# Moving a recurrence and half of an MLP from channels to tokens, and folding gate scores into other products, in a two-phase Trainium2 kernel

## Chip, cores and metric

The kernel runs on one core of a Trainium2 chip. The metric is the device time of one execution in microseconds (us), lower is better. "Granted clock" is the share of TensorE's full speed that the chip let it have; its two levels are 1.2 and 2.4 GHz, shown as 0.5 and 1.0.

## What is computed

The input is 16 x 56 x 56 tokens of 96 channels (50,176 tokens, fp32). The reference, cut to what matters:

```
x0 = x
x  = ln(x)                                  # over channels, no weights
w  = ln(x) * ln1_w + ln1_b                  # tokens in windows of 7x7 = 49 steps
h  = w[step] @ Bm + h @ A                   # recurrence over the 49 steps of a window
xr = h @ Cm
y  = gelu((ln(xr)*ln2_w + ln2_b) @ W1 + b1) @ W2 + b2     # 96 -> 384 -> 96
x2 = x0 + xr + y
t  = ln(x2)
scores = t @ gate_w + gate_b                # 4 experts, the two largest are kept
out = x2 + sum over the two kept experts of weight_e * (gelu(t @ w1_e + b1_e) @ w2_e + b2_e)
```

## The kernel before

**Phase 1** walks over 49 tiles; tile t holds step t of all 1,024 windows (8 groups of 128 tokens), so the recurrence runs from tile to tile. Five engines run queues that are written out by hand as loops over `periods()`; period p works on several tiles at once: the MLP of tile p, state and `xr` of tile r = p + 1, the input of tiles p + 2 and p + 3, gate and sorting of tiles p - 1 and p - 2. An engine takes its queue strictly in order, so a wait holds all that is behind it.

Per tile, in the kernel before:

- DVE takes moments of x (`moments(LN_X)`), POOL makes 1/sqrt(variance) with a `pow` (`rstd_of`, L396), ACT normalises x by tokens (L476), PE turns it to channels (`to_channels`, L878), ACT copies it out (L530).
- PE sums the new state by channels: `from_state` (L917, A) and `from_input` (L924, Bm), 2 products of 512 columns each; ACT copies it to `h_t` (L510). `sum_xr` (L931) multiplies it by Cm with tokens on the partitions, in 8 products; DVE copies `xr` out (L728), takes moments, normalises it (L626), PE turns it, ACT rounds it to `y_hi` (L501) and DVE makes the rest `y_lo` (L702). `y_hi` and `y_lo` are the two fp32r parts that `up` needs.
- `up` (L890 to L892) makes 6 units of 512 columns, three products each; ACT applies gelu (L486); `down` (L901) sums the units by channels in fp32; ACT adds the bias (L493), `turn_y` (L909) turns the sum to tokens, `add_x2` (L636) adds `x + xr`.
- LN over x2: moments, POOL's `pow`, `normalise` on DVE (L626, written into the row), PE turns it (L878), ACT copies it (L523), and 8 products of 4 columns (L976) give the scores. `gate` picks the two experts, `positions` gives each row its place among the 6 pairs of experts, and POOL scatters the rows to DRAM with 8 indirect DMAs (L405). A row is x2, t, the scores below the largest, and the token's number: 197 words.

**Phase 2** reads the sorted rows in 103 blocks of 512 tokens with one pair of experts each: turn t to channels (L1006), 6 units of `up2` (L1020 to L1022), gelu, `down2` (L1034 to L1036), turn back (L1043), combine (L833), scatter the result (L437).

Of the kernel before, what the change touches and what calls it, by code (L numbers as in the profile page):

```python
# [6 lines left out]
F32R = mybir.dt.float32r  # L7
# [27 lines left out]
COL_X2, COL_T, COL_BELOW, COL_ID = 0, C, 2 * C, 2 * C + EXPERTS  # L35
# [18 lines left out]
X_RING = 5  # L54
G_RING = 4
# [15 lines left out]
FIRST_LOADS, LATER_LOADS = 5, 3  # L71
PREP_STEPS = 9
# [7 lines left out]
def periods():  # L80
    return range(-3, TILES + 2)
# [1017 lines left out]
```

## Time and profile before

| | us |
|---|---|
| three runs | 2190.02, 2192.92, 2193.45 (median 2192.92) |
| the profiled execution: its time | 2187.12 |
| its span (first to last instruction) | 2185.4 |
| busy: PE, PEld, DVE, ACT, POOL | 2036.4, 1435.5, 1609.1, 1467.4, 1523.1 |
| mean granted clock | 0.981 |

Times of rows in the trace count from the start of the span. PEld is PE's loading of the stationary operand. A fp32 product shows as two records, so "x16" stands for 8 fp32 products; the shown end of a PE record is modelled and lies past the start of the next. "[1.78 <-DVE y_lo L702]" is idle time ahead of a row and what ended it.

### The profile page before, as it was taken

Reading aid. Unit: us, or ns where it says so; the run is one execution under the profiler, and the core shown is the slowest. Engines: PE = TensorE matmul, PEld = TensorE weight load, DVE = VectorE, ACT = ScalarE, POOL = GpSimd, SP = SyncE. Lnnn points to the kernel's source line nnn. Section 1 sums busy time; section 2 is a strip of 40 time slices with the busy share of each in tenths; the row PEclk is TensorE's granted clock in tenths of the full one; section 3 lists DMA queues with packets and bytes.
Section 4 is the critical chain, followed back from the end, with each engine's and each line's share of the span. In section 5 each row is a group of like instructions: output and inputs, shape, how many; then the busy total and the mean of one; then the engine's idle time right before and its main releaser. Section 6 shows DMA issues by size and latency. Waiting matters only on the chain.

```text
span 2185.4 us, 39186 instructions
## 1 busy us (share of the span) xinstructions
PE 2036.4 (93%) x10145; PEld 1435.5 (66%) x10145; DVE 1609.1 (74%) x6863; ACT 1467.4 (67%) x2529; POOL 1523.1 (70%) x1389
## 2 busy tenths in 40 slices
PE   3999999999999999999966999999999999999996
PEld 2666665656666666666644777777777777777775
DVE  5777777777777777777754777777777777777775
ACT  3555555555454555555524888888888888898895
POOL 2366666666666666666553777778888887788876
PEclk9999999999999999999967999999999999999998
DMA  4111111111111121211116767766666677666663
GB/s 160 32 51 59 53 58 54 57 56 49 63 49 62 47 64 48 63 49 47 36 45 201 213 199 208 213 203 200 204 200 208 199 208 209 206 209 211 207 203 94
DMA packets 120722, 272.90 MB, mean 125 GB/s; under 512 B 25702, under 2 KB 34303, under 8 KB 120500
## 3 DMA queue, kind: packets, MB, share of 16 engines
q1 hardware_dynamic: 85680, 209.91, 32.8%
q0 software_dynamic: 32000, 58.87, 7.6%
q8 instruction: 84, 1.38, 0.3%
q10 hardware_dynamic: 2820, 1.61, 0.3%
q14 instruction: 138, 1.13, 0.2%
HBM read 204.28 MB, written 66.98 MB: 124 GB/s over the span
## 4 chain that ended last, share of the span: by engine, by line
PE 53%; POOL 20%; DVE 19%; issue 6%; ACT 1%; DMA 1%; ACTq 0%; SPq 0%; POOLq 0%; DVEq 0%
POOL rstd L396 10%; POOL sorted_rows L405 7%; PE mix_ps L1034 7%; PE mix_ps L1036 6%; PE mix_ps L1035 6%; DVE xr_n L626 4%; PE turn_ps L1020 3%; PE up_ps L1020 3%; PE turn_ps L1022 3%; PE up_ps L1021 3%; PE turn_ps L1021 3%; PE up_ps L1022 3%; DVE stats L614 3%; PE tok_ps L1043 3%; DVE y_lo L702 3%
## 5 line engine op out<-in xcount | busy, mean ns | idle before, releaser
L437 POOL DMA_INDIRECT out<-out_sb,idx x412 | 440.1, 1068 | 199.2 <-issue 125.3
L789 DVE TENSOR_TENSOR g_lo<-g,g_hi 128x512 fp32r<-128x512 f32 x618 | 418.4, 687 | 167.4 <-ACT g_hi L547 93.6
L405 POOL DMA_INDIRECT sorted_rows<-rows,pos x392 | 421.1, 1074 | 114.0 <-issue 99.9
L547 ACT CAST g_hi<-g 128x512 fp32r<-128x512 f32 x618 | 380.9, 616 | 13.1
L426 POOL TENSOR_TENSOR ex<-euler,rows 128x8 f32<-128x8 f32 x206 | 367.8, 1798 | 13.6 <-DMA rows<-sorted_rows 12.5
L486 ACT ACTIVATE g<-up_ps 128x512 f32<-128x512 f32 x294 | 175.7, 598 | 250.7 <-PE up_ps L892 135.9
L901 PE MATMUL y_ps<-g,d_raw 128*96 128x512 f32 x588 | 302.3, 609 | 0.2 <-ACT y_sb L493 0.2
L396 POOL TENSOR_TENSOR rstd<-var_eps,neg_half 128x8 f32<-128x8 f32 x147 | 248.4, 1689 | 12.2
L1034 PE MATMUL mix_ps<-g_hi,ew 128*96 128x512 f32 x618 | 246.5, 399 | 1.8 <-DVE g_lo L789 1.2
L393 POOL TENSOR_SCALAR var_eps<-moment 128x8 f32<-128x8 f32 x147 | 31.8, 216 | 307.2 <-DVE moment L620 293.5
L1036 PE MATMUL mix_ps<-g_lo,ew 128*96 128x512 f32 x618 | 244.4, 396 | 0.0
L1035 PE MATMUL mix_ps<-g_hi,ew 128*96 128x512 f32 x618 | 244.0, 395 | 0.0
L890 PE MATMUL up_ps<-y_hi,w_hi 98*128 98x512 f32 x294 | 185.6, 631 | 25.5 <-DVE y_lo L702 25.1
L541 ACT ACTIVATE g<-turn_ps 128x512 f32<-128x512 f32 x310 | 184.5, 595 | 27.5 <-PE turn_ps L1022 17.9
L541 ACT ACTIVATE g<-up_ps 128x512 f32<-128x512 f32 x308 | 183.3, 595 | 22.8 <-PE up_ps L1022 11.3
L626 DVE TENSOR_SCALAR xr_n<-xr,moment,rstd 128x96 f32<-128x96 f32 x392 | 98.3, 331 | 117.3 <-POOL rstd L396 117.3
L493 ACT ACTIVATE y_sb<-y_ps,b_col 96x512 f32<-96x512 f32 x98 | 67.0, 684 | 166.4 <-PE y_ps L901 162.2
L559 ACT ACTIVATE y_sb<-mix_ps,ew 96x512 f32<-96x512 f32 x206 | 140.7, 683 | 48.3 <-PE mix_ps L1036 38.3
L476 ACT ACTIVATE x_n<-x_in,shift,rstd 128x96 f32<-128x96 f32 x392 | 149.7, 455 | 0.0
L1020 PE MATMUL turn_ps<-y_hi,ew 98*128 98x512 f32 x310 | 137.5, 444 | 1.4 <-DVE y_lo L794 1.4
L1020 PE MATMUL up_ps<-y_hi,ew 98*128 98x512 f32 x308 | 135.6, 440 | 3.1 <-DVE pair_of L844 3.1
L1036 PEld LDWEIGHTS mix_ps<-g_lo,ew 128*96 128x96 f32 x618 | 99.8, 161 | 43.2
(159 smaller groups left out, 4426.1 us busy)
## 6 DMA issues: line engine op xcount, KB each, us to landing
ew<-expert_w SPq DMA_DIRECT2D x206, 384.0 KB
ew<-expert_w SPq DMA_DIRECT2D x206, 288.5 KB
rows<-sorted_rows SPq DMA_DIRECT2D x103, 394.0 KB
x_in<-in_x SPq DMA_DIRECT2D x49, 384.0 KB
out<-out_sb,idx POOLq DMA_INDIRECT x412
sorted_rows<-rows,pos POOLq DMA_INDIRECT x392
sorted_rows<-pad_rows SPq DMA_DIRECT2D x11, 394.0 KB, 10.6
expert_w<-w_hi SPq DMA_DIRECT2D x4, 192.0 KB, 2.1
```

The source lines that it names most:

```text
L396: pool.tensor_tensor(rstd[:, k, t % 2, :], var_eps[:, k, :], neg_half[:, :], ALU.pow).then_inc(rstd_ok[k], 1)
L405: pool.indirect_dma_start(out=sorted_rows[:, :], out_offset=bass.IndirectOffsetOnAxis(ap=pos[:, r, s:s + 1], axis=0), in_=rows[:, r, s, :] ...
L426: pool.tensor_tensor(ex[:, b % 2, s:s + 2, :], euler[:, :].rearrange("p (s e) -> p s e", s=2), rows2[:, b % IN_RING, s:s + 2, COL_BELOW:CO ...
L437: pool.indirect_dma_start(out=out_rows, out_offset=bass.IndirectOffsetOnAxis(ap=idx[:, r, s:s + 1], axis=0), in_=out_sb[:, r, s, :], in_of ...
L541: act.activation(g[:, n % G_RING, :], up_bank(n), ACT.Gelu).then_inc(gelu2_done, 1)
L547: act.copy(g_hi[:, n % PART_RING, :], g[:, n % G_RING, :]).then_inc(hi_done, 1)
L789: dve.tensor_tensor(g_lo[:, n % PART_RING, :], g[:, n % G_RING, :], f(g_hi[:, n % PART_RING, :]), ALU.subtract).then_inc(lo_done, 1)
L901: pe.matmul(y_ps[0:C, :], d_raw[:, k, :], g[:, n % G_RING, :], start=(k == 0), stop=(k == KB - 1)).then_inc(down_done, 1)
L1020: pe.matmul(up_bank(n), hi[0:KR, :], t_hi, start=True, stop=False)
L1034: pe.matmul(y2_bank(q), hi, g_hi[:, part, :], start=(k == 0), stop=False)
L1035: pe.matmul(y2_bank(q), lo, g_hi[:, part, :], start=False, stop=False)
L1036: pe.matmul(y2_bank(q), hi, g_lo[:, part, :], start=False, stop=(k == KB - 1)).then_inc(down2_done, 1)
```

## The change

1. **x in two layouts.** Beside `x` the program gets `x_chan`, the same values with channels on the partitions (384 KB more per tile, by SyncE, ring of 2). Mean removal is folded into the weights (`in_w` is the centred Bm, and centred gate weights as 4 more columns), so `from_input` multiplies raw x in 8 products of 100 columns, and ACT multiplies the result by 1/std (`scale_in`). The transpose of normalised x and its copy go.
2. **State by tokens.** One product per group (`h_t` stationary, `state_aug` = A, Cm and Cm times the gate weights, 196 columns) gives the part of the next state and `xr` together. DVE adds the input's part (`take_state`), PE turns the state (`turn_h`), ACT copies it (`copy_h`). All of it goes in halves of 512 tokens.
3. **`xr` normalised on ACT.** ACT copies `xr` from PSUM and normalises it (`normalise_xr`), DVE only makes `shift`; POOL's `pow` for x (tile p + 4) and for `xr` (tile p + 1) is one instruction on 128x16 that waits for both variances. The small `var_eps` step moves from POOL to DVE.
4. **`down` by tokens.** Gelu's output is the stationary operand, 4 products of 100 columns per unit; b2 enters by one fp32r product of 400 columns per half. The bias copy and `turn_y` go. `add_x2` reads the sum directly.
5. **Scores as four more columns** of the products of 1, 2 and 4. They are summed in `gate_sum` (three small steps on ACT and DVE per half) and multiplied by 1/std of x2 in `gate`. L976, its transpose and copy go; t isn't written any more. `positions` comes one period earlier.
6. **Rows of 103 words**: x2, scores, mean, 1/std, number. Phase 2 normalises the block's rows on DVE (`normalise(b)`, 4 instructions of 128x96) two blocks ahead.

The core of the diff:

```diff
-COL_X2, COL_T, COL_BELOW, COL_ID = 0, C, 2 * C, 2 * C + EXPERTS
+COL_X2, COL_BELOW, COL_MEAN = 0, C, C + EXPERTS
+COL_RSTD, COL_ID = COL_MEAN + 1, COL_MEAN + 2
@@ SyncE
+            for t in range(XT_RING, TILES):
+                if t + X_RING - XT_RING - 1 >= X_RING and t + X_RING - XT_RING - 1 < TILES:
+                    load_x(t + X_RING - XT_RING - 1)
+                load_x_t(t)
@@ POOL, loop over periods
+            for p in periods():
+                if tile(p - 2):
+                    scatter(p - 2, (1,))
+                if tile(p - 1):
+                    rstd_t(p - 1)
+                if tile(p - 2):
+                    scatter(p - 2, (2, 3))
+                if tile(p + 4) or tile(p + 1):
+                    powers_of_variance(p + 4, p + 1)
+                if tile(p - 2):
+                    scatter(p - 2, (4, 5, 6, 7))
+                if tile(p - 1):
+                    scatter(p - 1, (0,))
@@ ACT, r = p + 1
+            def scale_in(t, h):
+                act.wait_ge(in_done, 2 * t + h + 1)
+                if h == 0:
+                    act.wait_ge(rstd_ok, rstd_calls(t, t - 3) + 1)
+                if t >= 1:
+                    act.wait_ge(h_tok_ok, 2 * (t - 1) + h + 1)
+                for s in range(HALF_SUBS):
+                    ins = act.activation(x_b[:, HALF_SUBS * h + s, :], in_ps[:, s, 0:C], ACT.Identity,
+                                         scale=rstd[:, rstd_calls(t, t - 3) % 2, LN_X, HALF_SUBS * h + s:HALF_SUBS * h + s + 1])
+                ins.then_inc(x_b_ok, 1)
+                act.copy(gate_sum[:, t % GATE_RING, HALF_SUBS * h:HALF_SUBS * (h + 1), :], in_ps[:, :, C:CG]).then_inc(in_gate_ok, 1)
...
+                if tile(r):
+                    copy_xr(r, 0)
...
+                if tile(p + 3):
+                    scale_in(p + 3, 0)
+                if tile(p):
+                    gelu(p, 4)
+                if tile(r):
+                    normalise_xr(r, 0)
+                if tile(p + 2):
+                    copy_h(p + 2, 0)
+                    copy_h(p + 2, 1)
+                if tile(r):
+                    normalise_xr(r, 1)
+                if tile(p):
+                    gelu(p, 5)
...
+                if tile(p + 3):
+                    scale_in(p + 3, 1)
+                if tile(r):
+                    y_high(r, 0)
@@ DVE, r = p + 1
+            def take_state(t, h):
+                subs = slice(HALF_SUBS * h, HALF_SUBS * (h + 1))
+                dve.wait_ge(state_done, 2 * (t + 1) + h + 1)
+                if tile(t):
+                    dve.wait_ge(xr_copied, 2 * t + h + 1)
+                if tile(t + 1):
+                    dve.wait_ge(x_b_ok, 2 * (t + 1) + h + 1)
+                    if t >= 0:
+                        dve.wait_ge(h_turned, 2 * t + h + 1)
+                    dve.tensor_tensor(h_tok[:, subs, :].rearrange("p (b s) c -> p b s c", b=2), state_ps[:, :, :, 0:C],
+                                      x_b[:, subs, :].rearrange("p (b s) c -> p b s c", b=2), ALU.add).then_inc(h_tok_ok, 1)
...
+                if tile(p):
+                    y_low(p, 1)
+                if tile(p - 1):
+                    add_x2(p - 1, 1)
+                    rows_stats(p - 1, 1)
+                    variance(LN_T, p - 1, (rstd_t_ok, p - 1))
+                if tile(r) or r == -1:
+                    take_state(r, 0)
+                if tile(p + 4):
+                    t = p + 4
+                    dve.wait_ge(x_loaded[t % X_RING], 16 * (t // X_RING + 1))
+                    for h in range(2):
+                        half_stats(LN_X, t, h, x_in[:, t % X_RING, :, :])
+                    variance(LN_X, t, (rstd_ok, rstd_calls(t - 1, t - 4) + 1))
...
+                if tile(r):
+                    xr_stats(r, 0)
+                if tile(r) or r == -1:
+                    take_state(r, 1)
+                if tile(r):
+                    xr_stats(r, 1)
+                    variance(LN_R, r, (rstd_ok, rstd_calls(r + 2, r - 1) + 1))
+                if tile(p - 1):
+                    gate(p - 1)
+                if tile(r):
+                    n = rstd_calls(r + 3, r)
+                    dve.wait_ge(rstd_ok, n + 1)
...
+                if tile(p):
+                    add_x2(p, 0)
+                if tile(p - 1):
+                    positions(p - 1)
+                if tile(r):
+                    if r >= 2:
+                        dve.wait_ge(x2_ok, 2 * (r - 1))
+                    dve.tensor_tensor(x_xr[:, r % 2, :, :], xr[:, :, :], x_in[:, r % X_RING, :, :], ALU.add).then_inc(x_xr_ok, 1)
+                if tile(p):
+                    rows_stats(p, 0)
+                if tile(r):
+                    y_low(r, 0)
@@ PE
+                if k == 0:
+                    tok.take(pe, x2_ok, 2 * t + h + 1)
+                    pe.matmul(tok_ps[:, 0:HALF_SUBS * CG], ones_r[:, :], b2_parts[:, :], start=True, stop=False)
+                pe.wait_ge(gelu_done, n + 1)
+                for s in range(HALF_SUBS):
+                    ins = pe.matmul(mlp_ps[:, s, :], g[:, n % G_RING, sub(s)], d_mlp[:, k, :], start=False,
+                                    stop=(k == KB - 1 and s == HALF_SUBS - 1))
+                ins.then_inc(down_done, 1)
...
+            def from_state(t, h):
...
+                for s in range(HALF_SUBS):
+                    ins = pe.matmul(state_ps[:, s // 2, s % 2, :], h_t[:, sub(HALF_SUBS * h + s)], state_aug[:, :], start=True, stop=True)
+                ins.then_inc(state_done, 1)
@@ phase 2, DVE
+            def normalise(b):
+                dve.wait_ge(rows_loaded[b % IN_RING], 16 * (b // IN_RING + 1))
+                if b >= 2:
+                    dve.wait_ge(t_turned, b - 1)
+                for s in range(BSUBS):
+                    row = rows2[:, b % IN_RING, s, :]
+                    ins = dve.tensor_scalar(t_tok[:, b % 2, s, :], row[:, COL_X2:COL_BELOW], row[:, COL_MEAN:COL_RSTD],
+                                            row[:, COL_RSTD:COL_ID], ALU.subtract, ALU.mult)
+                ins.then_inc(t_tok_ok, 1)
...
+                    if u == 3 and b + 2 < BLOCKS:
+                        normalise(b + 2)
```

(In `from_state` h_t's group is the stationary operand and `state_aug` moves; `y_high(p, 1)`, gelu 0 to 2 and the copies of `xr` open ACT's period.)

On PE, before, the end of a period and the start of the next (transposes are MATMUL rows with `ident`):

```order
L878 MATMUL turn_ps<-ident,x_n 96x128 x8
L976 MATMUL tok_ps<-gate_aug,tn_t 128x4 x8
L901 MATMUL y_ps<-g,d_raw 96x512 x2
L878 MATMUL turn_ps<-ident,xr_n 96x128 x8
L909 MATMUL tok_ps<-ident,y_sb 128x96 x4
L917 MATMUL mix_ps<-h_t,a_raw 96x512 x2
L890 MATMUL up_ps<-y_hi,w_hi 128x512
```

The same place with the change, from the second `from_input` to the next period's first `up` and `from_state`:

```order
L1060 MATMUL y_ps<-in_w,x_t 128x100 x4
L1030 MATMUL turn_ps<-ident,xr_n 96x128 x4
L1051 MATMUL tok_ps<-d_mlp,g 128x100 x4
L1030 MATMUL turn_ps<-ident,xr_n 96x128 x4
L1051 MATMUL tok_ps<-d_mlp,g 128x100 x4
L1040 MATMUL up_ps<-y_hi,w_hi 128x512
```

The product of the state (L917), which stood between the transpose of `xr` and the next `up`, has moved behind the first two units of `up`; two units' `down` in four small products each stand around the second transpose.

On ACT, before, a whole period from the first two gelus:

```order
L486 ACTIVATE g<-up_ps 128x512 x2
L476 ACTIVATE x_n<-x_in,shift,rstd 128x96 x4
L510 COPY h_t<-mix_ps 96x1024
L486 ACTIVATE g<-up_ps 128x512 x2
L476 ACTIVATE x_n<-x_in,shift,rstd 128x96 x4
L493 ACTIVATE y_sb<-y_ps,b_col 96x512
L486 ACTIVATE g<-up_ps 128x512
L523 COPY tn_t<-turn_ps 96x1024
L486 ACTIVATE g<-up_ps 128x512
L530 COPY x_t<-turn_ps 96x1024
L493 ACTIVATE y_sb<-y_ps,b_col 96x512
L501 CAST y_hi<-turn_ps 96x1024
```

With the change, the second part of a period, from the fourth gelu to the rounding of `y_hi` (its two halves stand on one row, the first closes the period and the second opens the next):

```order
L530 ACTIVATE x_b<-y_ps,rstd 128x96 x4
L533 COPY gate_sum<-y_ps 128x16
L569 ACTIVATE g<-up_ps 128x512
L554 ACTIVATE xr_n<-xr,shift,rstd 128x96 x4
L538 COPY h_t<-turn_ps 96x512 x2
L554 ACTIVATE xr_n<-xr,shift,rstd 128x96 x4
L569 ACTIVATE g<-up_ps 128x512
L530 ACTIVATE x_b<-y_ps,rstd 128x96 x4
L533 COPY gate_sum<-y_ps 128x16
L562 CAST y_hi<-turn_ps 96x512 x2
```

Behind the wait for `shift` (first L554) there now stand eight more steps that `y_hi` has to wait for, among them a `scale_in`; before, only L501 stood behind the transpose of `xr_n`.

## Rows read from the trace of the kernel before

**Rows 1.** The page's first part: busy time, share of the span, instructions.

```profile
span 2185.4 us, 39186 instructions
PE 2036.4 (93%) x10145; PEld 1435.5 (66%) x10145; DVE 1609.1 (74%) x6863; ACT 1467.4 (67%) x2529; POOL 1523.1 (70%) x1389
```

**Rows 2.** Windows: start:end, length, busy us (records), clock, DMA share, GB/s.

```profile
60.00:1080.00 1020.00, 959.49 (x4895) 632.47 (x4896) 774.65 (x4176) 546.38 (x924) 657.32 (x678) 1.00 0.17 53
1190.00:2150.00 960.00, 958.74 (x4776) 724.63 (x4775) 736.44 (x2293) 851.52 (x1493) 779.17 (x596) 1.00 0.69 205
```

**Rows 3.** Timeline, PE: start, us, engine, line; `up` of tile 0 and tile 48.

```profile
50.04 0.50 PE L890 MATMUL up_ps<-y_hi,w_hi 98*128 98x512 f32 x1
...
1105.30 0.50 PE L890 MATMUL up_ps<-y_hi,w_hi 98*128 98x512 f32 x1 [1.78 <-DVE y_lo L702]
```

**Rows 4.** Waits from 60 to 1080: engine line, releaser, us, times, longest.

```profile
PEld up_ps L890 <- DVE y_lo L702: 62.7, 46, 1.4
```

**Rows 5.** Timeline of one steady period, PE.

```profile
611.11 1.04 PE L878 MATMUL turn_ps<-ident,x_n 128*96 128x128 f32 x8
612.09 1.95 PE L976 MATMUL tok_ps<-gate_aug,tn_t 97*128 97x4 f32 x16
...
621.12 0.40 PE L890 MATMUL up_ps<-y_hi,w_hi 98*128 98x512 f32 x1
621.36 0.39 PE L891 MATMUL up_ps<-y_lo,w_hi 96*128 96x512 f32 x1
622.18 1.94 PE L924 MATMUL mix_ps<-x_t,b_aug 97*96 97x512 f32 x4
627.07 1.92 PE L931 MATMUL mix_ps<-a_raw,h_t 96*128 96x96 f32 x16
```

**Rows 6.** Timeline, DVE: a gate, statistics, and `y_lo` of 512 columns.

```profile
616.46 0.17 DVE L646 COPY score<-tok_ps 128x32 f32<-128x32 f32 x1
618.61 0.53 DVE L636 TENSOR_TENSOR rows<-tok_ps,x_xr 128x384 f32<-128x384 f32 x1
625.43 1.34 DVE L614 BATCH_NORM_STATS2 stats<-x_in 128x6 f32<-128x96 f32 x8
626.81 0.64 DVE L620 BATCH_NORM_AGGREGATE moment<-stats 128x2 f32<-128x6 f32 x8
1166.88 0.69 DVE L794 TENSOR_TENSOR y_lo<-y_ps,y_hi 96x512 fp32r<-96x512 f32 x1 [15.84 <-ACT y_hi L553]
```

**Rows 7.** Timeline, ACT.

```profile
621.32 1.29 ACT L486 ACTIVATE g<-up_ps 128x512 f32<-128x512 f32 x2 [2.54 <-issue]
622.51 1.53 ACT L476 ACTIVATE x_n<-x_in,shift,rstd 128x96 f32<-128x96 f32 x4
1166.26 0.58 ACT L553 CAST y_hi<-y_ps 96x512 fp32r<-96x512 f32 x1 [29.48 <-PE y_ps L1006]
```

**Rows 8.** Timeline, POOL, and a DVE row inside its pair of powers.

```profile
2.42 0.74 POOL L369 MEMSET pad_rows<- 128x788 f32 x1
603.80 1.67 POOL L396 TENSOR_TENSOR rstd<-var_eps,neg_half 128x8 f32<-128x8 f32 x1
1154.85 0.96 POOL L405 DMA_INDIRECT sorted_rows<-rows,pos  x1 [0.30 <-issue]
1703.04 3.95 POOL L426 TENSOR_TENSOR ex<-euler,rows 128x8 f32<-128x8 f32 x2
1704.82 0.68 DVE L789 TENSOR_TENSOR g_lo<-g,g_hi 128x512 fp32r<-128x512 f32 x1
```

**Rows 9.** Timeline: last store of expert weights; phase 2's first transposes.

```profile
35.57 0.45 SPq L296 DMA_DIRECT2D expert_w<-b_col  x1
...
1165.14 1.09 PE L1006 MATMUL y_ps<-ident,rows 128*96 128x128 f32 x4 [10.90 <-DMA rows<-sorted_rows]
```

**Rows 10.** PE idle at 64.75, and the granted clock after 1105.30.

```profile
66.25 1.05 PE L878 MATMUL turn_ps<-ident,xr_n 128*96 128x128 f32 x8 [1.50 <-DVE xr_n L626]
```

**Rows 11.** Windows, PE alone: length, busy, clock, DMA share, GB/s.

```profile
1107.00:1108.00 1.00, 1.00 (x4) 0.50 0.00 0
```

More of the change, by code:

```diff
@@ L54 @@
 X_RING = 5
+XT_RING = 2
+GATE_RING = 6
 G_RING = 4
@@ new lines, in normalise_xr @@
+            def normalise_xr(t, h):
+                if h == 0:
+                    act.wait_ge(shift_ok, t + 1)
+                if t >= 1:
+                    act.wait_ge(xr_turned, 2 * (t - 1) + h + 1)
+                for s in range(HALF_SUBS * h, HALF_SUBS * (h + 1)):
+                    ins = act.activation(xr_n[:, s, :], xr[:, s, :], ACT.Identity, bias=shift[:, s:s + 1],
+                                         scale=rstd[:, rstd_calls(t + 3, t) % 2, LN_R, s:s + 1])
+                ins.then_inc(xr_n_ok, 1)
@@ L912, in from_state @@
-            def from_state(r):
-                mix.take(pe, h_t_ok, r + 1)
-                if r >= 1:
-                    pe.wait_ge(h_t_ok, r)
-                    for h in range(2):
-                        pe.matmul(mix_ps[0:C, half(h)], a_raw[:, 0, :], h_t[:, half(h)], start=True, stop=False)
-            def from_input(r):
-                pe.wait_ge(x_t_ok, r + 1)
-                if r == 0:
-                    pe.wait_ge(bias_rows, 48)
-                for h in range(2):
-                    ins = pe.matmul(mix_ps[0:C, half(h)], b_aug[:, :], x_t[:, half(h)], start=(r == 0), stop=True)
-                ins.then_inc(h_summed, 1)
@@ new lines, in down, with from_input @@
+                ins.then_inc(down_done, 1)
+            def from_input(t, h):
+                inp.take(pe, in_gate_ok, 2 * t + h + 1)
+                if h == 0:
+                    pe.wait_ge(x_t_loaded[t % XT_RING], 16 * (t // XT_RING + 1))
+                for s in range(HALF_SUBS):
+                    ins = pe.matmul(in_ps[:, s, :], x_t[:, t % XT_RING, sub(HALF_SUBS * h + s)], in_w[:, :], start=True, stop=True)
+                ins.then_inc(in_done, 1)
+            def from_state(t, h):
+                if t == -1 and h == 0:
+                    pe.wait_ge(bias_rows, 16 * 4)
+                if t >= 0:
+                    pe.wait_ge(h_t_ok, 2 * t + h + 1)
+                n = 2 * (t + 1) + h
+                if n >= 1:
+                    pe.wait_ge(h_tok_ok, min(n, 2 * TILES))
+                if n >= 3:
+                    pe.wait_ge(state_gate_ok, n - 2)
+                for s in range(HALF_SUBS):
+                    ins = pe.matmul(state_ps[:, s // 2, s % 2, :], h_t[:, sub(HALF_SUBS * h + s)], state_aug[:, :], start=True, stop=True)
+                ins.then_inc(state_done, 1)
@@ L941, in _ @@
                     up(p, 1)
-                if tile(p - 2):
-                    tok.take(pe, base_set, p - 1)
-                    pe.wait_ge(score_counted, p - 1)
-                    pe.matmul(tok_ps[:, 0:TYPES], earlier[:, :], count[:, :, SUBS - 1], start=True, stop=True)
-                    pe.matmul(tok_ps[:, TYPES:2 * TYPES], ones[:, :], count[:, :, SUBS - 1], start=True, stop=True).then_inc(
-                        ranked, 1)
-                if tile(r):
-                    from_input(r)
+                if tile(r) or r == -1:
+                    from_state(r, 0)
                 if tile(p):
```

471 lines of the change are left out of this document (241 added, 230 removed).

## Prediction

> **What bounds the kernel now.** First the page's busy shares: PE leads with 93% [rows 1]. Then the windows, to see whether that holds in both phases: in steady phase 1 PE is busy 959.49 of 1020 us and DVE only 774.65, in steady phase 2 PE is busy 958.74 of 960 with ACT next at 851.52; the clock is 1.00 in both [rows 2]. Then the timeline: `up` of tile 0 starts at 50.04 and that of tile 48 at 1105.30 [rows 3], so a period lasts 1055.3 / 48 = 21.98 us. The waits show how little PE idles in it: the largest, for `y_lo` ahead of `up`, is 62.7 us in 46 times, 1.4 us a period [rows 4]. So both phases go at PE's pace. A change that takes work from PE can shorten phase 1 until another chain takes over; phase 2 can only stay or get longer, since its PE work stays.
>
> **PE's work per period.** A fp32 product of 512 columns shows as two records, four records in 1.94 [rows 5], 0.43 each after the modelled tail. With tokens as the stationary operand, 16 records take 1.92 at 96 moving columns and 1.95 at 4 columns [rows 5]: 0.12 each whatever moves, so the loading sets it. Gone: four products of 512 columns for the state (3.5), six for `down` (5.2), Cm's 8 (1.9), the scores' 8 (1.95), three sets of 8 transposes at 1.04, `turn_y` (1.0): 16.7. New: 24 small products for `down` at two records (5.8), 8 `from_input` (1.9), 8 `from_state`, whose 196 columns I cost by columns, 2 x 0.43 x 196/512 = 0.33 each (2.6), two sets of transposes (2.1), b2 (0.4): 12.8. PE falls by about 3.9 to some 17.5 a period. PE would let phase 1 gain 48 x 4 = 190 us. It won't, since the order of waits now closes a longer loop over the other engines.
>
> **The loop that sets the new period.** Count from the moment at which half 0 of `y_lo` of tile p is there (0).
>
> - PE: two units of `up`, six products 0.24 apart [rows 5], 1.45; first half of `from_state` 1.3, seen 0.2 later: 2.95. DVE has done half 1 of `y_lo`, `add_x2`, statistics and variance of the rows by 2.7, so it waits here.
> - ACT copies half of `xr` (384 columns; 512 take 0.58 [rows 7]), 0.5: 3.5. DVE `take_state`: 0.53 for 384 columns as L636 [rows 6], and a small step 0.1: 4.2.
> - DVE, statistics of x for tile p + 4: 1.34 and 0.64 for the whole tile [rows 6], with one more stop between halves 2.1, variance 0.25: 6.55. Half of `xr`'s statistics 1.05, `take_state` 0.65, the other half 1.05, variance 0.25: 9.55.
> - POOL: the `pow` on 128x16, 3.15 (below): 12.75. Beside it runs `gate`: 2.15 before (616.46 to 618.61) [rows 6], with four small steps more and one less 2.55, so it ends at 12.1 and isn't what `shift` waits for. `shift` 0.25: 13.0.
> - ACT: half of `normalise_xr` 1.53 (as L476 [rows 7]), two `copy_h` of 0.6, other half 1.53, gelu 5 0.65 (two in 1.29 [rows 7]), `scale_in` 1.53 and 0.2, half of `y_hi` 0.6: 7.25, at 20.25.
> - DVE: half of `y_lo`, 0.69 [rows 6] and a handover: 21.05. PE starts the next `up` at 21.1.
>
> DVE's other work of the period (about 4 us between `shift` and `y_lo`, 15.6 in all) and ACT's 13.6 have room. POOL has 8 scatters of 0.96 plus 0.30 [rows 8], 10.1, and 1.67 + 3.15 of powers: 15, and comes to the 128x16 `pow` at about 7. So the loop, not a full engine, sets 21.1: 0.9 less than now, 48 x 0.9 = **-42 us**. Handing over in halves is what the change gains from, and the eight steps ahead of `y_hi` on ACT are what eats it.
>
> **The price of the 128x16 pow** isn't in the trace. Below it is bounded by 1.67 of the 128x8 one [rows 8] (nothing makes double the work cheaper), above by twice that, 3.34. POOL's plainest row takes 0.74 for 788 elements a partition [rows 8], so elements cost there, and little of 1.67 can be fixed cost; I take 3.15. At 1.67 the loop would close over `gate` instead, 0.65 earlier: 20.45.
>
> The Trainium skill (SBUF — State Buffer, "SBUF: two separate sides") says that VectorE and GpSimd share a port pair as an exclusive lock, held for the whole instruction, against a DVE instruction with two SBUF inputs. `gate` begins with such instructions right as the long `pow` starts. The row speaks against it: inside a pair of powers of 3.95 us a two-input DVE instruction took 0.68 [rows 8], where a wait for a power of nearly 2 would show. By the row the sum stays; by the rule it would be the third rival.
>
> **Start and end of phase 1.** Today the last of 20 stores of expert weights is issued at 35.57 [rows 9] and x for the first tiles is long there. Now x_t of tile 2 stands behind these stores in SyncE's queue, they start only after `later_weights`, which now stands behind the first `take_state` (about 33), and `from_input` of tile 2 stands ahead of the first transpose of `xr` on PE. That puts the first `up` at about 57: **+7 us** (between -2, if the stores come no later than today, and +12). At the other end 59.8 us lie between the last first `up` (1105.30) and phase 2's first transposes (1165.14) [rows 3, 9]. Normalising, transposing, copying and scoring the last tile go, and `positions` comes earlier; then POOL's queue is last: from about 10.5 on, 16 scatters at 1.26 and a `pow`, to 32.5, and as today 9.3 from its last scatter (1154.85 and 0.96 [rows 8]) to the transposes: 42, **-18 us** (-12 to -20).
>
> **Phase 2.** A block takes 9.8 us at PE's pace. `normalise` adds 1.0 to DVE's 7.5 (736.44 in 98 blocks [rows 2]). It stands two blocks ahead and `part_lo` three units ahead of its product, so its cover is about 3 units of 1.6; I cost it at 0. If the cover were gone, a block would grow by up to 1.0, 100 us; a tenth of that, 10, is my upper bound, since DVE stays at 87%. Rows of half the bytes relieve transfers that nothing waits for.
>
> **Sum.** Against the profiled execution's 2187.1: -42 + 7 - 18 + 0 = 2134. The median of the runs lies 5.8 above that execution: **2140 us**. Differences within 0.2% (4.4 us) are about what a measurement can't tell from no change.
>
> **Rivals.**
>
> 1. *The clock falls in the new gap; slower.* Between PE's last `down` of a period (18.9, after gelu 5) and the next `up` (21.1) there are 2.2 us of idle PE, in every period. For: after 1.78 idle at 1105.30 the clock was 0.50 by 1107 [rows 3, 11]. Against: 1.50 idle at 64.75 was followed by transposes at full speed, eight in 1.05 [rows 10], and ahead of 1105.30 PE had been slow already. At half clock the two `up` and the first `from_state`, 2.75, stand at the head of the loop and cost 2.75 more. In half the periods that is +66, 2206; in all, 2272. It decides from some 18 of 48 periods on. Chance 0.25.
> 2. *The pow of 128x16 costs like one of 128x8.* For: nothing but the comparison of rows says it is linear. Against: that comparison. 48 x 0.65 = 31 less: 2109. Chance 0.17.
> 3. *DVE stands still for the long pow.* `gate`'s first instruction waits until 12.75 and `shift` comes at 15.5 in place of 13.0: +2.5 a period, 2260. For: the skill's rule alone; against: the row above. Chance 0.05.
> 4. *The gain is used up by hand-overs.* The loop has 14 of them, and I gave most 0.05 to 0.1; with 0.05 more each and `normalise` showing 10 in phase 2 it is 0.7 a period, 2184. Chance 0.10.
>
> **How the numbers follow.** My forecast has 0.43. Faster by over 0.2% (below 2188.5): the forecast, rival 2, most of rival 4, and the part of rival 1 with few falls: 0.68. Within: 0.06. Slower: 0.26. The range leaves out the full forms of rivals 1 and 3 and goes below rival 2 by the early start and the larger gain at the end: 2095 to 2215; the forecast's own range is 2120 to 2165.
>
> **What would show it.** Right: first `up` of consecutive tiles 21 us apart; PE idle ahead of `up` for `y_lo` about 2.2; ACT's chain `normalise_xr` to `y_hi` 7 us without a gap; DVE's `shift` waiting for POOL; the new `pow` near 3.1; phase 2 blocks still 9.8. Wrong: clock under 1.00 in 60 to 1000, DVE waiting elsewhere (for PE at the second `take_state`), `gate` stretched, or PE waits for `g_lo` in phase 2.

## Result and the profile after

The changed kernel takes 2249.3 us (median of 4) against 2191.7: ratio 1.0265, interval 1.0251 to 1.0279. It is **slower by 2.65%** where I forecast 2140 us. The profiled executions have spans of 2248.0 and 2185.4. First the page's busy shares, which answer to [rows 1], then the windows that answer to [rows 2]:

```profile
PE 2013.8 (90%) x10865; PEld 1643.5 (73%) x10865; DVE 1583.5 (70%) x7089; ACT 1461.7 (65%) x3019; POOL 1581.4 (70%) x1147
```

```profile
60.00:1080.00 1020.00, 935.18 (x5624) 839.36 (x5624) 679.10 (x4021) 545.45 (x1415) 572.25 (x454) 0.89 0.20 55
1200.00:2220.00 1020.00, 956.63 (x4698) 708.56 (x4696) 798.36 (x2639) 846.18 (x1468) 911.90 (x587) 1.00 0.58 171
```

Two things stand out. In phase 1 the granted clock is 0.89 where it was 1.00. In phase 2 PE is busy 94% where it was full, and POOL, at 81% before [rows 2], now has 89%. The timeline of PE gives the marks that answer to [rows 3, 9]: the first `up`, that of tile 48, and phase 2's first transposes.

```profile
64.98 0.50 PE L1040 MATMUL up_ps<-y_hi,w_hi 98*128 98x512 f32 x1 [1.46 <-DVE y_lo L754]
...
1100.93 0.47 PE L1040 MATMUL up_ps<-y_hi,w_hi 98*128 98x512 f32 x1
...
1147.22 0.88 PE L1146 MATMUL y_ps<-ident,t_tok 128*96 128x128 f32 x3 [12.10 <-DVE t_tok L950]
```

So the 62.6 us between the spans come apart as: start +14.9; 48 periods 1035.95 in place of 1055.26, -19.3; end of phase 1 46.3 in place of 59.8, -13.5; phase 2 1100.8 in place of 1020.3, **+80.5**.

**Phase 1.** Where the clock falls shows in PE's timeline of one period, with the windows of 1 us beside it (length, PE busy, granted clock, DMA share, GB/s):

```profile
628.75 1.04 PE L1030 MATMUL turn_ps<-ident,h_tok 128*96 128x128 f32 x8
630.27 0.36 PE L1114 MATMUL y_ps<-count,earlier 128*128 128x6 f32 x2 [0.49 <-DVE count L797]
630.49 0.37 PE L1115 MATMUL y_ps<-count,ones 128*128 128x6 f32 x2
631.70 0.51 PE L1048 MATMUL tok_ps<-b_parts,ones_r 2*128 2x400 f32 x1 [0.85 <-DVE gate_sum L742]
632.14 2.03 PE L1051 MATMUL tok_ps<-d_mlp,g 128*128 128x100 f32 x8
633.87 0.77 PE L1040 MATMUL up_ps<-y_hi,w_hi 98*128 98x512 f32 x1
```

```profile
629.00:630.00 1.00, 0.78 (x8) 1.00 0.00 0
630.00:631.00 1.00, 0.58 (x4) 1.00 0.00 0
631.00:632.00 1.00, 0.30 (x1) 0.98 0.00 0
632.00:633.00 1.00, 1.00 (x5) 0.50 0.15 53
...
638.00:639.00 1.00, 1.00 (x8) 0.60 0.05 13
639.00:640.00 1.00, 1.00 (x11) 1.00 0.16 50
```

PE waits for `count`, the last step of `gate`, runs the two small rank products, and waits again for `gate_sum`, the second half of `add_x2`, which DVE reaches only behind `shift`. Then it runs at half clock (1.2 GHz) for some 6.8 us: `down`'s eight records take 2.03 in place of 1.03. The chain of waits shows both as PE's largest; rival 1's gap ahead of `up` isn't among them:

```profile
PE tok_ps L1048 <- DVE gate_sum L742: 46.1, 56, 1.8
...
PE y_ps L1114 <- DVE count L797: 34.5, 46, 1.4
```

From one first `up` to the next it takes 22.0, 20.5, 22.6, 23.7, again and again up to tile 27; a few later periods take 19.4.

**Phase 2.** POOL and DVE of one block, from POOL's timeline and DVE's:

```profile
1707.58 1.03 POOL L485 DMA_INDIRECT out<-out_sb,idx  x1 [0.18 <-issue]
1708.92 1.33 POOL L485 DMA_INDIRECT out<-out_sb,idx  x1 [0.30 <-issue]
1710.56 1.02 POOL L485 DMA_INDIRECT out<-out_sb,idx  x1 [0.30 <-issue]
1711.88 2.64 POOL L485 DMA_INDIRECT out<-out_sb,idx  x1 [0.30 <-issue]
1714.54 3.29 POOL L474 TENSOR_TENSOR ex<-euler,rows 128x8 f32<-128x8 f32 x2
```

```profile
1708.72 1.28 DVE L915 TENSOR_TENSOR g_lo<-g,g_hi 128x512 fp32r<-128x512 f32 x2
1709.93 1.05 DVE L950 TENSOR_SCALAR t_tok<-rows 128x96 f32<-128x96 f32 x4
1710.88 0.99 DVE L969 SCALAR_TENSOR_TENSOR out_sb<-tok_ps,weight,rows 128x96 f32<-128x96 f32 x4
1711.79 1.89 DVE L915 TENSOR_TENSOR g_lo<-g,g_hi 128x512 fp32r<-128x512 f32 x3
1713.59 0.68 DVE L920 TENSOR_TENSOR y_lo<-y_ps,y_hi 96x512 fp32r<-96x512 f32 x1
...
1717.86 0.19 DVE L928 TENSOR_TENSOR both<-ex,pair_of 128x32 f32<-128x32 f32 x1 [2.09 <-POOL ex L474]
```

POOL has no idle moment but the 0.18 to 0.30 of issue: 6.0 for four scatters, 3.3 for the powers and 1.1 of issue make 10.4, the block. One scatter in each block takes 2.64, beside three `g_lo` that run back to back, and one 1.33, beside two. DVE then waits 2.09 for the powers, falls behind with its `g_lo`, and does them in a row again: as I read it, the pattern feeds itself. Of the 412 scatters 99 take over 2.0, one in nearly every block. The least, median and longest of all out-scatters, before and after:

```profile
L437 POOL DMA_INDIRECT out<-out_sb,idx x412: 964/1034/1427, 1191.6 to 2175.6; - x138
```

```profile
L485 POOL DMA_INDIRECT out<-out_sb,idx x412: 967/1041/2767, 1175.9 to 2238.2; - x138
```

### The profile page after: what moved, and what is told of

The parts are those of the page before. It is cut to its first block, busy times and chain, and to the rows that moved or that the text cites. A ratio compares the mean times of both kernels' runs of the same rounds, so it can differ in the third digit from the quotient of the medians.

```text
span 2248.0 us, 41456 instructions
## 1 busy us (share of the span) xinstructions
PE 2013.8 (90%) x10865; PEld 1643.5 (73%) x10865; DVE 1583.5 (70%) x7089; ACT 1461.7 (65%) x3019; POOL 1581.4 (70%) x1147
## 4 chain that ended last, share of the span: by engine, by line
POOL 39%; issue 24%; PE 21%; DVE 9%; ACT 3%; another core or an unknown queue 1%; DMA 1%; SPq 1%; POOLq 0%; ACTq 0%; DVEq 0%
POOL out L485 27%; PE tok_ps L1051 7%; POOL rstd L437 6%; POOL ex L474 4%; PE turn_ps L1030 3%; DVE stats L703 3%; PE y_ps L1060 3%; PE mix_ps L1075 2%; POOL sorted_rows L451 2%; DVE moment L707 2%; PE up_ps L1040 1%; PE up_ps L1042 1%; PE up_ps L1041 1%; DVE h_tok L726 1%
## 5 line engine op out<-in xcount | busy, mean ns | idle before, releaser
L485 POOL DMA_INDIRECT out<-out_sb,idx x412 | 613.6, 1489 | 135.8 <-issue 112.4
L616 ACT CAST g_hi<-g 128x512 fp32r<-128x512 f32 x618 | 382.2, 618 | 13.1
L1051 PE MATMUL tok_ps<-d_mlp,g 128*128 128x100 f32 x2352 | 360.5, 303 | 3.1 <-issue 3.1
L1051 PEld LDWEIGHTS tok_ps<-d_mlp,g 128*128 128x128 f32 x2352 | 336.9, 219 | 24.5 <-issue 23.5
L1174 PE MATMUL mix_ps<-g_hi,ew 128*96 128x512 f32 x618 | 252.8, 409 | 65.8 <-issue 35.9
L437 POOL TENSOR_TENSOR rstd<-var_eps,neg_half 128x16 f32<-128x16 f32 x52 | 157.1, 3022 | 163.2 <-issue 97.6
L442 POOL TENSOR_TENSOR rows<-var_eps,neg_half 128x8 f32<-128x8 f32 x49 | 82.3, 1679 | 236.2 <-DVE var_eps L714 236.2
L754 DVE TENSOR_TENSOR y_lo<-turn_ps,y_hi 96x512 fp32r<-96x512 f32 x98 | 67.1, 686 | 243.3 <-issue 126.8
L554 ACT ACTIVATE xr_n<-xr,shift,rstd 128x96 f32<-128x96 f32 x392 | 151.8, 462 | 84.7 <-DVE shift L854 84.7
L1174 PEld LDWEIGHTS mix_ps<-g_hi,ew 128*96 128x96 f32 x618 | 99.5, 161 | 132.6 <-issue 59.5
L1075 PE MATMUL mix_ps<-state_aug,h_t 97*128 97x196 f32 x800 | 156.1, 339 | 2.0 <-DVE gate_sum L731 1.4
L1060 PEld LDWEIGHTS y_ps<-in_w,x_t 96*128 96x128 f32 x784 | 138.0, 250 | 21.2 <-ACT gate_sum L533 6.4
```

Of the source, the lines that this page charges most:

```text
L437: pool.tensor_tensor(rstd[:, n % 2, :, :], var_eps[:, LN_X:LN_T, :], neg_half[:, :].rearrange("p (k s) -> p k s", k=2), ALU.pow).then_inc( ...
L485: pool.indirect_dma_start(out=out_rows, out_offset=bass.IndirectOffsetOnAxis(ap=idx[:, r, s:s + 1], axis=0), in_=out_sb[:, r, s, :], in_of ...
L616: act.copy(g_hi[:, n % PART_RING, :], g[:, n % G_RING, :]).then_inc(hi_done, 1)
L1051: ins = pe.matmul(mlp_ps[:, s, :], g[:, n % G_RING, sub(s)], d_mlp[:, k, :], start=False, stop=(k == KB - 1 and s == HALF_SUBS - 1))
L1060: ins = pe.matmul(in_ps[:, s, :], x_t[:, t % XT_RING, sub(HALF_SUBS * h + s)], in_w[:, :], start=True, stop=True)
L1174: pe.matmul(y2_bank(q), hi, g_hi[:, part, :], start=(k == 0), stop=False)
```

## The experiments

The table has, from each profiled execution, the first `up`, the mean of 48 periods, phase 2's first transposes, and the mean block (starts of POOL's powers, block 10 to 90); the last column is the median of the timed runs. (One of one_pow's four took 2100.7; the other three have a median of 2054.2. single_source was timed once.) Before, measured again beside them, was 2188.3 to 2189.4.

| kernel | first up | period | phase 2 from | block | median |
|---|---|---|---|---|---|
| before | 50.0 | 21.98 | 1165.1 | 9.66 | 2191.7 |
| changed | 65.0 | 21.58 | 1147.2 | 10.44 | 2249.3 |
| no_normalise | 64.5 | 20.52 | 1089.3 | 9.65 | 2119.3 |
| before_scale | 49.2 | 21.95 | 1160.8 | 10.26 | 2242.1 |
| before_scale_u2 | 50.4 | 21.99 | 1164.5 | 9.69 | 2186.8 |
| psum_source | 65.6 | 20.57 | 1093.7 | 9.53 | 2121.4 |
| single_source | 64.8 | 20.87 | 1107.0 | 10.20 | 2181.7 |
| early_only | 64.2 | 20.59 | 1094.0 | 10.25 | 2178.8 |
| fill_gaps | 64.7 | 19.44 | 1039.6 | 10.26 | 2119.5 |
| rank_behind | 65.8 | 19.50 | 1042.8 | 10.26 | 2124.8 |
| norm_in_wait | 64.3 | 19.49 | 1040.7 | 9.65 | 2065.7 |
| t_in_row | 64.8 | 19.43 | 1041.6 | 9.68 | 2067.1 |
| one_pow | 65.8 | 19.46 | 1040.5 | 9.54 | 2056.2 |
| best_fill | 64.1 | 19.38 | 1035.0 | 9.54 | 2047.4 |

### Phase 2: is it the normalising?

**no_normalise** (ratio to before 0.9696, 0.9679 to 0.9712) leaves the normalising out:

```diff
-                pe.wait_ge(t_tok_ok, b + 1)
+                pe.wait_ge(rows_loaded[b % IN_RING], 16 * (b // IN_RING + 1))
...
-    ins = pe.transpose(y_ps[0:C, sub(s)], t_tok[:, b % 2, s, :], ident[:, :])
+    ins = pe.transpose(y_ps[0:C, sub(s)], rows2[:, b % IN_RING, s, COL_X2:COL_BELOW], ident[:, :])
...
-                    if u == 3 and b + 2 < BLOCKS:
-                        normalise(b + 2)
```

> Leaves the normalising of phase 2 out: the transposes read x2 of the row itself, all else of the changed kernel stays. Phase 2 of the changed kernel takes 1100.8 us where it took 1020.3 before. Theory A (the four instructions of normalise a block on DVE push the g_lo subtractions together, and POOL's scatter beside them stands still, 2.64 for 0.97): the long scatter is gone, a block goes from 10.42 back to about 9.8 and the kernel to 2249 - 75 = 2175, range 2160 to 2190. Rival B (the narrower rows, or where they lie in memory, slow the scatters and loads): still 2249, long scatters still there.

Phase 2 takes 1022 us again, the block 9.65, and no scatter is over 1.49. Theory A holds for phase 2 and B falls: the rows are the narrow ones. But the kernel came out 56 us below my figure, since phase 1, whose code is that of the changed kernel, took 58 us less. early_only, below, takes that up.

**before_scale** (1.0251, 1.0234 to 1.0268) adds the four instructions to the kernel before:

```diff
+            def scale_rows(b):
+                dve.wait_ge(rows_loaded[b % IN_RING], 16 * (b // IN_RING + 1))
+                for s in range(BSUBS):
+                    row = rows2[:, b % IN_RING, s, :]
+                    dve.tensor_scalar(t_tok[:, b % 2, s, :], row[:, COL_X2:COL_T], row[:, COL_BELOW:COL_BELOW + 1],
+                                      row[:, COL_BELOW + 1:COL_BELOW + 2], ALU.subtract, ALU.mult)
...
+                    if u == 3 and b + 2 < BLOCKS:
+                        scale_rows(b + 2)
```

> The kernel before with one thing added: four DVE tensor_scalar of 128x96 from the rows into a tile that nobody reads, at the place in the block where the changed kernel normalises. Theory A: block 9.8 to about 10.4, scatters of 2.6 appear once a block, the kernel 2192 + 60 to 80 = 2262. Rival B (narrow rows): 2192, since the rows here are as wide as before. Rival C (DVE's added load matters only together with an end of phase 1 or a row layout of the changed kernel): 2192 to 2210.

```profile
L438 POOL DMA_INDIRECT out<-out_sb,idx x412: 969/1040/2767, 1187.4 to 2227.9; - x138
```

The long scatters appear, and 54 us with them. One part of the change, put alone into the old kernel, makes 57 of the 80.5 us that phase 2 lost (2237.7 - 1160.8 = 1076.9). The rest is the difference between blocks of 10.26 and 10.44, which also shows between kernels whose phase 2 is the same code (fill_gaps, early_only and the changed one). It goes with the number of long scatters: 71 over 2.0 in before_scale, fill_gaps and early_only, 99 in the changed kernel. Why they come in more blocks there stays open.

### What holds the scatter up, and does the place count?

**before_scale_u2** (0.999, 0.998 to 0.9999) is before_scale with `scale_rows(b + 2)` at `u == 2`, right ahead of `weights(b)`.

> The kernel before with the same four added DVE instructions as before_scale, at u 2 right ahead of the weights, in place of u 3. If the place decides: block 9.65, total within 8 us of 2190, no scatter of 2.6. If DVE's load decides: 10.25 and 2242 as before_scale.

The same work costs nothing there: it lies in DVE's wait for POOL's powers, no `g_lo` is pushed onto its neighbours, and no scatter is over 1.45.

**psum_source** (0.971, 0.9674 to 0.9746), of the changed kernel, normalise at `u == 3`; the subtraction of `g_hi` is left out:

```diff
-                dve.tensor_tensor(g_lo[:, n % PART_RING, :], g[:, n % G_RING, :], f(g_hi[:, n % PART_RING, :]),
-                                  ALU.subtract).then_inc(lo_done, 1)
+                dve.tensor_scalar(g_lo[:, n % PART_RING, :], up_bank(n), 1e-4, 0.0, ALU.mult, ALU.add).then_inc(lo_done, 1)
```

> The changed kernel with g_lo of phase 2 made by one DVE tensor_scalar of 128x512 that reads PSUM (the up product) and no SBUF (g - g_hi is left out), about 0.68 as before: DVE's load and order stay, only where the operand comes from changes. Normalise stays at u 3. Theory A (POOL's scatter stands still beside DVE instructions whose sources all lie in SBUF): no scatter over 1.1, block 9.65, phase 2 back to 1020. Rival (DVE is late, whatever it reads): scatters of 2.6 and a block of 10.3 to 10.4 remain.

```profile
L485 POOL DMA_INDIRECT out<-out_sb,idx x412: 966/972/1049, 1121.9 to 2094.4; - x138
```

```profile
L474 POOL TENSOR_TENSOR ex<-euler,rows x206: 1625/1648/1704, 1092.6 to 2082.1; 128x8 f32<-128x8 f32 x103
```

```profile
L915 DVE TENSOR_SCALAR g_lo<-turn_ps x310: 668/686/693, 1099.1 to 2085.6; 128x512 fp32r<-128x512 f32 x155
```

These are its scatters, its powers and half of its `g_lo`; of the changed kernel the same row of `g_lo`:

```profile
L915 DVE TENSOR_TENSOR g_lo<-g,g_hi x618: 673/685/695, 1152.7 to 2229.4; 128x512 fp32r<-128x512 f32 x155
```

DVE's instruction is as long, 0.686 and 0.685, and stands at the same place of the program; its one source is PSUM, where it had two in SBUF. Not one of 412 scatters is over 1.05, and the powers, up to 2.07 in the changed kernel, stay under 1.71. That alone doesn't exclude DVE's lateness, since no scatter has three `g_lo` in a row beside it here. But three scatters have two `g_lo` beside them that lie in time just as those beside the changed kernel's scatter at 1708.92, which took 1.33; one of them, from POOL's timeline and DVE's:

```profile
1400.41 0.97 POOL L485 DMA_INDIRECT out<-out_sb,idx  x1 [0.30 <-issue]
```

```profile
1400.20 0.68 DVE L915 TENSOR_SCALAR g_lo<-turn_ps 128x512 fp32r<-128x512 f32 x1
1400.80 0.68 DVE L915 TENSOR_SCALAR g_lo<-up_ps 128x512 fp32r<-128x512 f32 x1
```

All three took 0.97, and the 98 that lie so in the changed kernel 1.31 to 1.34. So it isn't DVE's load or lateness by itself: a `g_lo` that reads SBUF holds POOL off.

**single_source** (one run, 2181.7) makes `g_lo` of two one-source instructions that read SBUF; here too the subtraction is left out:

```diff
...
+                dve.tensor_scalar(unread[:, n % 2, :], g[:, n % G_RING, :], 1.0, 0.0, ALU.mult, ALU.add)
+                dve.tensor_scalar(g_lo[:, n % PART_RING, :], g[:, n % G_RING, :], 1e-4, 0.0, ALU.mult, ALU.add).then_inc(lo_done, 1)
```

> The changed kernel with g_lo of phase 2 made by two DVE tensor_scalar of 128x512 that read g alone (the subtraction of g_hi is left out), in place of one instruction with two SBUF inputs; normalise stays. DVE has as much or more to do for each g_lo. Theory A1 (POOL's scatter stands still beside a DVE instruction with two SBUF inputs only): scatters all at 0.97 to 1.05, pow pairs at 3.29, blocks at 9.8 or less. Theory A2 (one SBUF source is enough to hold POOL off): scatters beside g_lo still at 1.3 to 2.6. Theory A3 (the port has nothing to do with it, DVE's load is what delays POOL): scatters as in the changed kernel.

```profile
L486 POOL DMA_INDIRECT out<-out_sb,idx x412: 966/1035/2951, 1135.2 to 2170.2; - x138
```

A2: one SBUF source is enough, at least in this form: each of the two took 0.41 for 512 columns, against 0.69 from PSUM. Yet the four of normalise, also from SBUF but 96 columns wide, don't hold a scatter up at this place, as the timelines of POOL and of DVE in psum_source show:

```profile
1706.24 0.97 POOL L485 DMA_INDIRECT out<-out_sb,idx  x1 [0.30 <-issue]
```

```profile
1706.10 1.14 DVE L949 TENSOR_SCALAR t_tok<-rows 128x96 f32<-128x96 f32 x4
```

(In before_scale_u2 and norm_in_wait the scatter beside them takes up to 1.13 and 1.12, 0.1 more than one with nothing beside it.)

The Trainium skill (SBUF — State Buffer, "SBUF: two separate sides") says that VectorE and GpSimd share a port pair which one side holds for a whole instruction. It ties the standstill of a DMA issued by GpSimd to a VectorE instruction in a two-port mode, during which GpSimd can't write the descriptors; for an instruction with two SBUF inputs it has the lock hold only against a GpSimd instruction that reads SBUF. These runs agree that scatters stand still beside VectorE's reads of SBUF: up to 2.95 in single_source, and nothing over 1.05 once the source is PSUM. They go further in one point: `g_lo` with two SBUF inputs, in the changed kernel, holds a scatter up as well, to 2.77.

### Phase 1: what does the clock cost?

**fill_gaps** (0.9684, 0.9668 to 0.9701) and **rank_behind** (0.9713, 0.9697 to 0.9729). The first gives PE something to do:

```diff
+            def keep_busy(dst):
+                for _ in range(3):
+                    pe.matmul(dst, ident[:, :], ident[:, 0:C], start=True, stop=True)
...
                     inp.take(pe, base_set, p)
+                    keep_busy(y_ps[:, 416:416 + C])
                     pe.wait_ge(score_counted, p)
...
                 if tile(p):
+                    pe.wait_ge(gelu_done, UNITS * p + 4)
+                    keep_busy(up_ps[:, 1, 0:C])
                     down(p, 3)
```

> The changed kernel with PE given work to do while it waits: three products of 128x96 on the identity ahead of the rank products and three behind them, 0.78 each set, results overwritten. No wait is removed and nothing else moves. Theory D: clock 0.98 or more over 60 to 1080, period about 20.2, the kernel 2249 - 65 = 2184. Rival E: within 15 us of 2249. Rival F (the clock falls because of the gap ahead of up, as I predicted, and not of this one): clock stays at 0.89, time grows by up to 48 x 0.5.

The second removes the waits: PE does `down(p, 3)` ahead of the rank products, and DVE does `add_x2(p, 0)` inside `gate`, behind the comparisons.

> The changed kernel with one order changed in phase 1: PE does down 3 ahead of the rank products, and DVE's first add_x2 stands inside gate, ahead of shift. That takes the two waits (0.75 for count, 0.8 for gate_sum a period) out of PE's middle. Theory D (these waits let the clock fall, and the 7 to 11 us at half speed that follow cost some 3.5 us in most periods): granted clock over 60 to 1080 from 0.89 to 0.98 or more, period from 21.58 to about 20.0, the kernel 2249 - 75 = 2174. Rival E (the period is set by the loop over POOL's pow and ACT, and slow PE is only slack): the clock rises but the kernel stays within 15 us of 2249.

The windows 60 to 980 of fill_gaps, of rank_behind, and of early_only (told below):

```profile
60.00:980.00 920.00, 895.45 (x6194) 809.06 (x6194) 675.25 (x4023) 538.62 (x1415) 572.40 (x455) 0.99 0.22 61
```

```profile
60.00:980.00 920.00, 847.22 (x5612) 748.65 (x5610) 673.96 (x4006) 534.69 (x1406) 568.40 (x450) 0.99 0.22 60
```

```profile
60.00:980.00 920.00, 858.04 (x5317) 774.48 (x5318) 643.64 (x3821) 517.22 (x1338) 537.83 (x428) 0.91 0.21 59
```

Work thrown in front of a waiting PE makes the kernel 130 us faster, 108 of them in phase 1. Nothing that PE waits for was moved or taken away, so the waits are not what costs; the half clock behind them is. Taking them away does the same. D holds, with more gain in phase 1 than the 65 to 75 I gave it (my 20.0 to 20.2 for a period at full clock was 19.4); E and F fall. The other 23 us are the block of 10.26.

**early_only** (0.996, 0.9945 to 0.9974) loads x_t of tile 2 ahead of the 20 stores of expert weights and changes nothing else:

```diff
+            load_x_t(XT_RING)
             sp.wait_ge(later_prep, 2)
...
-            for t in range(XT_RING, TILES):
+            for t in range(XT_RING + 1, TILES):
```

> The changed kernel with only x_t of tile 2 loaded ahead of the stores. Nothing in phase 1's loop changes. First up at 63.5, 1.5 earlier. If the pattern of clock falls hangs on how the start of the loop lies in time, phase 1's mean period moves (between 20.5 and 21.6, as in no_normalise and single_source, whose phase 1 is the changed kernel's); if it hangs on the loop alone, 21.58 stays and the kernel takes 2247.

The first `up` came 0.8 earlier, and the kernel 70 us. Phase 1 settles into periods of 20.5 in place of the cycle of four; so does it in no_normalise, psum_source and single_source, whose phase 1 is the changed kernel's too. So one loop has several steady patterns of falls, and small things pick one: 20.5 to 21.6 a period, 50 us. Between the two profiled executions, 76 us apart, phase 1 up to the first transposes gives 53 and phase 2 (block 10.25) 23. Not even an edit is needed: psum_source's four executions take 2105.9 to 2134.1 at a mean clock of 0.944 to 0.933, and its row in the table is of the shortest.

### Together

**norm_in_wait** (0.9435, 0.942 to 0.9451) is rank_behind with x_t early and `normalise(b + 2)` at `u == 2` ahead of `weights(b)`. **t_in_row** (0.9445, 0.9429 to 0.9461) normalises in phase 1 instead, on DVE behind `x_xr`, and carries t in the row. **one_pow** (0.9391, 0.9369 to 0.9412) is norm_in_wait with one `pow` of 128x16 a block:

```diff
-                for s in range(0, BSUBS, 2):
-                    pool.tensor_tensor(ex[:, b % 2, s:s + 2, :], ..., ALU.pow).then_inc(ex_ok, 1)
+                pool.tensor_tensor(ex[:, b % 2, :, :], ..., rows2[:, b % IN_RING, :, COL_BELOW:COL_MEAN], ALU.pow).then_inc(ex_ok, 2)
```

> rank_behind with two orders more: x_t of tile 2 is loaded ahead of the 20 stores of expert weights on SyncE, and phase 2's normalise stands right ahead of the weights (u 2) and not at u 3, so that it lies in DVE's wait of 2.1 for POOL's pow. Start: first up at 57 to 59 (65.8 in rank_behind), or still 62 to 65 if b_col's late landing and not the store queue sets it. Phase 2, theory A (what hurts is that three g_lo stand in a row beside the fourth scatter): no 2.6 scatter, block 9.65 to 9.8, 10.26 in rank_behind, -45 to -55; total 2125 - 7 - 50 = 2068. Rival (any added DVE work does it, wherever it stands): block stays at 10.2 to 10.4, total 2118.

> rank_behind with x_t of tile 2 early and the normalising done in phase 1 again, now on DVE (eight instructions of 128x96 behind x_xr), rows 96 values wider; phase 2 as in the kernel before. Phase 1: DVE has 4 us idle a period there, so 0 to +0.5 a period, 0 to +24. Phase 2: block 9.65, -58 against rank_behind. Total 2125 - 7 - 58 + 0 to 24 = 2060 to 2084. Rival: y_low stands behind these instructions on DVE, and they come back in full, +2.1 a period, 2160.

> norm_in_wait with the two pow of 128x8 a block made one of 128x16 (3.00 against 3.29 measured). If POOL bounds phase 2 there, 0.3 a block less, -29 against norm_in_wait; if PE bounds it again, within 5 us of it.

norm_in_wait came within 3 us of its figure: block 9.65, no scatter over 1.40, PE full again. Its start came at 64.3: not 57 to 59, but in the 62 to 65 that I had given as the other case. t_in_row ties with it, so phase 1 has room for this work as well. one_pow's profiled execution is 11.4 shorter, under half of the 29 that it would be if POOL alone were the bound. PE shows 910.00 of 910 us busy (1090 to 2000) in both, at blocks of 9.65 and 9.54: a PE row that looks full does not say that PE alone sets the pace.

**best_fill** (0.9353, 0.9338 to 0.9369) is fill_gaps with three of these edits, x_t early, `normalise(b + 2)` ahead of the weights and the one `pow`:

> fill_gaps with x_t early, normalise ahead of the weights and one pow of 128x16 a block. Phase 1 as fill_gaps (period 19.44), phase 2 as one_pow (block 9.54): 2119.5 - 1.5 - 61 = 2055, within 6 us of one_pow.

```profile
PE 1946.6 (95%) x11453; PEld 1618.9 (79%) x11453; DVE 1591.7 (78%) x7089; ACT 1452.3 (71%) x3019; POOL 1428.7 (70%) x1044
```

2047.4 us: 6.5% under the kernel before and 9% under the changed one, with the change's idea kept.

## Why the prediction was wrong

**"I cost it at 0", phase 2: the step that failed; +80.5 measured.** I asked what DVE's added 1.0 does to PE, by way of `part_lo`, and found cover enough. I never asked what it does to POOL, whose scatters it pushes beside rows of `g_lo`. POOL at 779 of 960 [rows 2] looked free; but the 0.30 of issue behind each scatter [rows 8] isn't in that share; with 1.1 of it in each of 99 blocks it makes 886 of 960, 92%. My upper bound was a tenth of 1.0 a block; it grew by 0.8. This term alone took the kernel out of my range: without it, it would have come out at about 2169. That both phases went at PE's pace was wrong too: psum_source and one_pow, with the same PE work in phase 2, take 1010.5 and 1011.9 for it, where the kernel before took 1020.3.

**The weighing of the Trainium skill's rule was half done.** I read that `g_lo` took 0.68 inside a pair of powers of 3.95 [rows 8] as evidence against a lock. It is only evidence that DVE doesn't wait for `pow`. The other side stood in the same row: two powers of 1.67 are 3.34, not 3.95. POOL was the one that stood still, and psum_source, where no power is over 1.71, shows what for. Rival 3, DVE standing still for the long `pow`, fell: that `pow` mostly takes 3.0, and `gate` beside it isn't stretched.

**"-42 us" for 48 periods; measured -19.3.** Two errors of opposite sign, and it is luck that the sum lies so near. The loop itself is shorter than mine, 19.44 (fill_gaps) and not 21.1. ACT's timeline in fill_gaps, in a period that begins at 612.72:

```profile
615.75 0.48 ACT L545 COPY xr<-mix_ps 128x384 f32<-128x384 f32 x1 [0.73 <-PE mix_ps L1075]
...
625.48 1.54 ACT L554 ACTIVATE xr_n<-xr,shift,rstd 128x96 f32<-128x96 f32 x4 [1.56 <-DVE shift L854]
626.93 1.04 ACT L538 COPY h_t<-turn_ps 96x512 f32<-96x512 f32 x2
627.87 1.54 ACT L554 ACTIVATE xr_n<-xr,shift,rstd 128x96 f32<-128x96 f32 x4
629.31 0.58 ACT L569 ACTIVATE g<-up_ps 128x512 f32<-128x512 f32 x1
629.79 1.01 ACT L530 ACTIVATE x_b<-y_ps,rstd 128x96 f32<-128x96 f32 x4
630.68 0.17 ACT L533 COPY gate_sum<-y_ps 128x16 f32<-128x16 f32 x1
630.74 1.08 ACT L562 CAST y_hi<-turn_ps 96x512 fp32r<-96x512 f32 x2
```

`copy_xr` ends at 3.5 as predicted, ACT gets `shift` at 12.8 (13.0 to 13.1 predicted), and the six steps ahead of `y_hi` take 5.26, not 6.65: `scale_in`, which reads PSUM and has no bias, takes 1.01, and I had taken the 1.53 of a row that reads SBUF with a bias (which of the two counts, no run shows); neighbours overlap by 0.1. That is worth 48 x 1.66 = 80 us that I didn't forecast. The clock took it back: 21.58 - 19.44 = 2.14 a period, 103 us.

**Rival 1, the clock.** The sign and size were right (+66 to +132 for the falls, 103 measured) and I gave it 0.25; the place was wrong. I looked for one long gap and followed only the loop. The gap that counts is off the loop: `down(p, 3)` waits for an `add_x2` that stands behind `shift`, and so behind POOL's `pow`, on DVE. And the falls cost in the whole of the stretch behind them, not in the two `up` at the head.

**Start +7; measured +14.9.** The mechanism (x_t of tile 2 behind the 20 stores) was seen, but cost 3.3 of wait on PE and 1.5 at most of the start (65.8 to 64.3): with x_t early, PE waits for `xr_n` instead. The rest lies in a longer chain, at half clock, through weights, two states and the long `pow`. **End of phase 1 -18; measured -13.5**, and -18 in fill_gaps (1039.6 - 997.9 = 41.7). **The `pow` of 128x16**, 3.15 predicted, takes 3.0; rival 2 falls. **Rival 4**, hand-overs: the loop had none of that loss.

**Figures that don't follow from their rows**, and that the sum doesn't rest on: the 62.7 of [rows 4] is a wait of PEld; PE itself waits 23.0 for `y_lo` and 37.1 for `xr_n` there. "Some 17.5" for PE's new period fits neither 21.98 - 3.9 = 18.1 nor its busy 20.7 - 3.9 = 16.8; rank_behind shows 847.22 of 920, 18.0 a period. And a block took 9.66 before, not 9.8.

## What to carry over

Before work is added to an engine with room, look at what it does to the *order in time* of its long instructions against the other engine that shares its port: placed in a wait that exists anyway, the same four instructions cost nothing; one unit further on they cost 54 us. Count an in-order queue's issue gaps as busy before calling it free. And trace every wait of PE to its releaser, also off the loop: a PE that waits twice for 0.8 us can lose more to the clock than to the waits, and filling such a wait with work that is thrown away is a test (and a cure) that takes a few lines.

## What the hardware showed that I had not expected

- A POOL scatter of 0.97 takes up to 2.77 beside DVE's `g_lo` of 128x512 from SBUF, and at most 1.05 beside the same length of work from PSUM. POOL's `pow` of 128x8 stretches too, from 1.63 to 2.20 (kernel before). DVE hardly stretches: its `g_lo` with two SBUF inputs takes 0.68, and 0.82 at most (one_pow).
- DVE instructions of 128x96 from SBUF hold a scatter up by 0.1 at most, 512 columns by much more. Scatters beside two `g_lo` take 1.3, beside three with `y_lo` behind them 2.64: why not in proportion stays open, and so does whether `y_lo`, with one operand in PSUM, takes part.
- It also counts where they lie. In the kernel before, 132 scatters had one `g_lo` that began inside them and took 0.97 to 0.98; the 32 where a `g_lo` had begun 0.2 earlier and a second followed at once took 1.30 to 1.34.
- The same loop of phase 1 ran at 20.5, 20.6, 20.9 or 21.6 us a period in kernels that differ outside it. A difference of 50 us between two kernels can be a pattern of clock falls that neither edit asked for: compare stretches at equal granted clock.
